# A three-layer CIN on one core: the matmuls of zeros at the start are removed

## The chip, the cores and the metric

The kernel runs on one core of one Trainium2 chip. The metric is device time in microseconds (us) of one execution; lower is better. The kernel before takes 562.39 us, the median of three runs that lie between 562.30 and 562.44 us.

## The reference

A compressed interaction network (CIN) over 512 examples, 39 fields and embeddings of 16. Each layer multiplies the original fields with the current maps, pair by pair, and contracts all pairs with a weight tensor:

```python
for idx, (W, b) in enumerate(params):                      # three layers, 128 outputs each
    z = jnp.einsum('bhd,bkd,hks->bsd', x0, xk, W) + b[None, :, None]
    z = jax.nn.relu(z)
    if idx != n_layers - 1:
        half = z.shape[1] // 2
        xk = z[:, :half, :]                                # 64 maps go on
        direct.append(z[:, half:, :])                      # 64 go to the output
    else:
        direct.append(z)
logit = jnp.sum(jnp.concatenate(direct, axis=1), axis=-1)  # sum over the 16
```

All data is float32. The einsum has 39 x 39 pairs in layer 0 (780 distinct ones) and 39 x 64 in layers 1 and 2.

## The kernel before, in words

**Tiling.** The 512 x 16 columns are cut into 16 chunks of 512 columns. For one chunk and one layer, VectorE (DVE) forms products of a field with a map, 128 pairs on the partitions by 512 columns, and TensorE (PE) contracts these 128 rows with 128 x 128 weights into the PSUM tile z. Two such tiles form a "couple". Layer 0 has seven tiles, so four couples, the last with a single tile; layers 1 and 2 have 20 tiles, ten couples each.

**Kinds of couples.** A couple is of kind E (exact), S or D (split). For E, DVE writes float32 products to the ring `exact` of four places, and PE multiplies them in float32; the profile shows each such 512-column matmul of a tile as two weight loads and two matmul records, so a couple is four records. For S and D the products are split into a high and a low part by ScalarE (ACT) and by GpSimd (POOL) or DVE, and PE runs three faster matmuls for a tile. Chunk 0 is nearly all E, and so are the first two couples of layer 0 of chunk 1 (`EARLY = 2`).

**Order of work.** Each engine has its own list of instructions, and semaphores between them. PE contracts, in order: layer 0 of chunk 0 (four couples), the two early couples of layer 0 of chunk 1, then for each chunk c layer 1 of c, the last couples of layer 2 of chunk c-1, layer 0 of chunk c+1, and layer 2 of c. Once layer 0 of a chunk is contracted, ACT applies bias and ReLU (lines 675 and 679) and writes the maps twice; only then can DVE form the products of layer 1.

**The start.** SP issues the loads of the fields (line 337) and of the weights of layer 0 (line 358), and ACT issues one part of these weights (line 699). DVE sums the two halves of the weights of layer 0 as they land (line 476), and forms the products of couple 0 and couple 1 between those sums (line 426). PE waits for each couple's products with `exact_ready`, and for `w0_summed`.

**What the change touches.** `WARM = 3` (line 72), the semaphore `warm_ready` (line 255), a memset of the tile `final` by DVE (line 479), and in PE's list ahead of the first contraction a wait and three float32 matmuls of that tile with itself, all zeros, into `z[2]` (lines 618 to 620). Their result is used by nobody: the first real matmul into `z[2]` starts a new accumulation. `final` is next written by ACT at line 696, late in chunk 1.

Of the kernel before, what the change touches and what calls it, by code (L numbers as in the profile page):

```python
# [7 lines left out]
OUT = 128  # L8
# [60 lines left out]

WEIGHT_CUTS = (0, 4, 8, 12, 16, TILES)  # L70
WEIGHTS_AHEAD = 1
WARM = 3

SUM_LAST_AT = 6
SUM_DIRECT_AT = 6
# [134 lines left out]
def cin_kernel(nc, x_fields, x_spread, w0, w1, w2, b, out):  # L210
# [7 lines left out]
    with ctx:  # L218
        def sb(name, shape, dt=fp32):
            return ctx.enter_context(nc.sbuf_tensor(name, shape, dt))  # L220

        def pb(name, shape):
            return ctx.enter_context(nc.psum_tensor(name, shape, fp32))

        def sem(name):
            return ctx.enter_context(nc.semaphore(name))
# [15 lines left out]
        final = sb("final", [128, COLS])  # L242
# [5 lines left out]
        z = [pb(f"z{n}", [128, COLS]) for n in range(3)]  # L248
# [3 lines left out]
        d_raw = pb("d_raw", [128, 2, COLS])  # L252

        w0_loaded = [sem(f"w0_loaded{p}") for p in range(W0_PARTS)]
        warm_ready = sem("warm_ready")
        w0_summed = sem("w0_summed")
        w_loaded = [None] + [[sem(f"w{n}_loaded{p}") for p in range(len(WEIGHT_CUTS) - 1)] for n in (1, 2)]
        weights_hi = [sem(f"weights{n}_hi") for n in range(3)]
# [27 lines left out]
        def wait_contracted(engine, layer, c):  # L286

            what, _, _, k = LAST_STEP[layer, c]
            if what == "exact":
                engine.wait_ge(exact_used, PLACE[E][layer, c, k] + 1)  # L290
            else:
                engine.wait_ge(lo_used, USED[layer, c, k] + 1)
# [99 lines left out]
        def _(dve):  # L392
# [83 lines left out]
                nc.vector.tensor_tensor(w_exact[0][:, a:e, :], w0_staged[:, a:e, 0, :], w0_staged[:, a:e, 1, :],  # L476
                                        ALU.add).then_inc(w0_summed, 1)

            nc.vector.memset(final[:, :], 0.0).then_inc(warm_ready, 1)
            for p in range(W0_PARTS):  # L480
                sum_weights0(p)
                multiply(0, 0, range(p, p + 1))
# [26 lines left out]
        def _(pool):  # L509
# [13 lines left out]
            def weights_split_lo(n, tiles):  # L523

                while split[n] < len(RUNS[n]) and RUNS[n][split[n]][1] < tiles:
                    _, a, e = RUNS[n][split[n]]
                    split[n] += 1
                    m = SPLIT_TILES[n].index(a)
                    e = min(e, TILES - 1)
                    pool.wait_ge(weights_hi[n], split[n])  # L530
                    nc.gpsimd.tensor_tensor(w_lo[n][:, m:m + e - a, :], w_exact[n][:, a:e, :],  # L531
                                            w_hi[n][:, m:m + e - a, :].bitcast(fp32),
                                            ALU.subtract).then_inc(weights_lo[n], 1)
# [24 lines left out]
        def _(pe):  # L558
            def contract(layer, c, couples):
                for step in SCHEDULES[SEGMENTS.index((layer, c, couples))]:  # L560
# [21 lines left out]
                    if layer and c <= 1:  # L582
                        if what == "exact":
                            pe.wait_ge(w_loaded[layer][k // 2], 16)
                        elif what == "hi":
                            pe.wait_ge(weights_lo[layer], 1 + [a <= 2 * k < e for _, a, e in RUNS[layer]].index(True))
                            if k == COUPLES[layer] - 1:
                                pe.wait_ge(weights_last_lo[layer], 1)
# [25 lines left out]
                    if what != "hi":  # L614
                        mm.then_inc(exact_used if what == "exact" else lo_used, 1)


            pe.wait_ge(warm_ready, 1)
            for _ in range(WARM):
                nc.tensor.matmul(z[2][:, :], final[:, 0:OUT], final[:, :], start=True, stop=True)  # L620
            contract(0, 0, range(COUPLES[0]))
            contract(0, 1, range(EARLY))
            for c in range(CHUNKS):
# [152 lines left out]
```

## Time and profile before

| | |
|---|---|
| median of the runs (562.30 to 562.44) | 562.39 us |
| the profiled execution's own time | 562.33 us |
| its span, first to last instruction | 560.5 us |
| TensorE busy | 551.9 us, 98% |
| VectorE busy | 535.9 us, 96% |
| GpSimd busy | 499.5 us, 89% |
| ScalarE busy | 379.4 us, 68% |
| share of TensorE in the chain that ended last | 82% |

The profile shows one execution. PE stands for matmuls, PEld for weight loads, which run beside them; SPq and ACTq are DMA issues. A "record" is one line of PE or PEld; the start of a matmul is measured, its end is modelled and includes the time in which the array drains, so two neighbours overlap a little. The pace of a stretch is therefore read from the distance between starts. Idle time that stands in brackets behind an instruction is what its engine was idle just before it, and the arrow names what ended the wait.

### The profile page before, as it was taken

The numbers are of one execution on the slowest core, as the hardware profiler recorded it, in microseconds if no ns is written. First come the engines' busy times: TensorE is split into PE (matmuls) and PEld (weight loads), VectorE is DVE, ScalarE is ACT, GpSimd is POOL, SyncE is SP. The second block draws the span as 40 slices with busy tenths as digits, with TensorE's granted clock in tenths as the row PEclk, the third lists the DMA queues.
The fourth block names the chain that finished last, engine by engine and source line by source line (L and its number), as shares of the span: only waits on it lengthen the run. The fifth ranks groups of instructions, "written<-read, shape, count | busy, mean of one in ns | idle before, by whom it ended". The sixth has DMA issues, their size and how long they took to land.

```text
span 560.5 us, 6190 instructions
## 1 busy us (share of the span) xinstructions
PE 551.9 (98%) x2008; PEld 374.9 (67%) x2008; DVE 535.9 (96%) x496; ACT 379.4 (68%) x427; POOL 499.5 (89%) x228
## 2 busy tenths in 40 slices
PE   7999999999999999999999999999999999999997
PEld 2435667667677677777767677677777767677665
DVE  4679999999999999999999999999999999999985
ACT  0436577776858767676776858777676876858662
POOL 0438899899999989999899999989999899999986
PEclk9999999999999999999999999999999999999999
DMA  8997391844828266391845828276391845826200
GB/s 326 418 408 317 132 370 34 325 191 181 344 87 331 108 254 271 146 361 30 331 183 183 342 95 333 98 262 263 150 363 29 333 177 192 333 99 215 81 1 20
DMA packets 21056, 122.17 MB, mean 218 GB/s; under 512 B 2720, under 2 KB 2976, under 8 KB 10784
## 3 DMA queue, kind: packets, MB, share of 16 engines
q1 hardware_dynamic: 20736, 121.51, 56.0%
q8 instruction: 16, 0.26, 0.2%
q10 hardware_dynamic: 288, 0.26, 0.2%
q14 instruction: 16, 0.13, 0.1%
HBM read 121.24 MB, written 0.52 MB: 217 GB/s over the span
## 4 chain that ended last, share of the span: by engine, by line
PE 82%; DVE 10%; issue 3%; ACT 2%; DMA 1%; POOL 1%; SPq 0%; DVEq 0%; POOLq 0%; ACTq 0%
PE z L611 82%; DVE raw L426 4%; DVE exact L426 3%; DVE d_raw L426 2%; DMA fields<-x_fields 1%; DVE lo L440 1%; POOL lo L515 1%; ACT hi L656 1%; ACT maps L675 0%; ACT final L696 0%; ACT L675 0%; DVE sums L453 0%; DVE sums L447 0%; SPq L358 0%; SPq L337 0%
## 5 line engine op out<-in xcount | busy, mean ns | idle before, releaser
L515 POOL TENSOR_TENSOR lo<-raw,hi 128x1024 fp32r<-128x1024 f32 x198 | 469.1, 2410 | 12.1 <-ACT hi L656 11.6
L656 ACT ACTIVATE hi<-raw 128x1024 fp32r<-128x1024 f32 (+1 forms) x213 | 219.1, 1029 | 125.1 <-DVE raw L426 112.0
L611 PE MATMUL z<-hi,w_hi 128*128 128x512 f32 (+1 forms) x559 | 220.8, 399 | 0.9 <-ACT hi L656 0.4
L426 DVE TENSOR_TENSOR raw<-spread,maps 128x1024 f32<-128x1024 f32 x184 | 219.0, 1210 | 2.1 <-ACT maps L675 2.1
L611 PE MATMUL z<-hi,w_lo 128*128 128x512 f32 x513 | 202.5, 395 | 0.0
L611 PE MATMUL z<-lo,w_hi 128*128 128x512 f32 x544 | 196.7, 451 | 0.2 <-POOL lo L515 0.2
L611 PE MATMUL z<-exact,w_exact 128*128 128x512 f32 (+1 forms) x386 | 180.4, 594 | 2.8 <-DVE exact L426 2.0
L611 PEld LDWEIGHTS z<-lo,w_hi 128*128 128x128 f32 x544 | 101.2, 188 | 56.2 <-issue 31.5
L611 PEld LDWEIGHTS z<-hi,w_hi 128*128 128x128 f32 (+1 forms) x559 | 104.8, 188 | 31.4 <-ACT final L696 3.7
L611 PEld LDWEIGHTS z<-exact,w_exact 128*128 128x128 f32 (+1 forms) x386 | 72.1, 189 | 68.0 <-issue 53.7
L611 PEld LDWEIGHTS z<-hi,w_lo 128*128 128x128 f32 x513 | 96.2, 188 | 22.9 <-issue 0.5
L426 DVE TENSOR_TENSOR exact<-spread,maps 128x1024 f32<-128x1024 f32 x76 | 91.4, 1212 | 8.2 <-ACT maps L675 5.7
L656 ACT ACTIVATE hi<-d_raw 128x1024 fp32r<-128x1024 f32 x74 | 75.8, 1025 | 21.5 <-DVE d_raw L426 18.7
L440 DVE TENSOR_TENSOR lo<-d_raw,hi 128x1024 fp32r<-128x1024 f32 x74 | 89.9, 1215 | 0.0
L426 DVE TENSOR_TENSOR d_raw<-spread,maps 128x1024 f32<-128x1024 f32 x60 | 73.3, 1221 | 0.5
L675 ACT ACTIVATE maps<-z,bias 64x512 f32<-64x512 f32 x64 | 41.5, 648 | 3.4 <-PE z L611 2.2
L515 POOL TENSOR_TENSOR hi<-raw,hi 12x512 fp32r<-12x512 f32 x15 | 19.2, 1279 | 18.5 <-ACT hi L656 18.4
L531 POOL TENSOR_TENSOR w_lo<-w_exact,w_hi 128x512 fp32r<-128x512 f32 (+3 forms) x10 | 9.9, 1001 | 22.7 <-ACT w_hi L665 22.7
L426 DVE TENSOR_TENSOR raw<-fields,copies 76x512 f32<-76x512 f32 (+1 forms) x29 | 27.1, 934 | 0.0
L679 ACT ACTIVATE direct<-z,bias 64x512 f32<-64x512 f32 x32 | 21.9, 685 | 0.8
L426 DVE TENSOR_TENSOR exact<-fields,copies 128x1024 f32<-128x1024 f32 x15 | 18.2, 1212 | 0.0
L426 DVE TENSOR_TENSOR d_raw<-fields,copies 128x1024 f32<-128x1024 f32 x14 | 17.1, 1222 | 0.0
(21 smaller groups left out, 69.6 us busy)
## 6 DMA issues: line engine op xcount, KB each, us to landing
spread<-x_spread SPq DMA_DIRECT2D x80, 1024.0 KB, 8.1
fields<-x_fields SPq DMA_DIRECT2D x31, 768.0 KB, 6.8
fields<-x_fields SPq DMA_DIRECT2D x15, 512.0 KB, 5.6
w_exact<-w SPq DMA_DIRECT2D x10, 256.0 KB, 14.7
spread<-x_fields SPq DMA_DIRECT2D x1, 768.0 KB, 10.1
raw<-w SPq DMA_DIRECT2D x1, 640.0 KB, 6.7
spread<-x_fields SPq DMA_DIRECT2D x1, 512.0 KB, 10.7
out<-sums SPq DMA_DIRECT2D x2, 240.0 KB, 4.2
```

The costliest lines, as they stand in the source:

```text
L426: nc.vector.tensor_tensor(products, by_field, by[0:rows, :].unsqueeze(1).to_broadcast([rows, tiles, COLS]), ALU.mult).then_inc(ready, 1)
L440: nc.vector.tensor_tensor(low_part(layer, c, k), d_raw[low_rows(layer, k), 0:tiles_in(layer, k), :], hi[low_rows(layer, k), place % HI_RIN ...
L515: nc.gpsimd.tensor_tensor(low_part(layer, c, k), raw[low_rows(layer, k), PLACE[S][layer, c, k] % RAW_RING, 0:tiles_in(layer, k), :], hi[lo ...
L531: nc.gpsimd.tensor_tensor(w_lo[n][:, m:m + e - a, :], w_exact[n][:, a:e, :], w_hi[n][:, m:m + e - a, :].bitcast(fp32), ALU.subtract).then_ ...
L611: mm = nc.tensor.matmul(z_of(layer, c)[:, :], w[0:rows, :], part[0:rows, :], start=(step == FIRST_STEP[layer, c] and p == 0), stop=(step = ...
L656: nc.scalar.activation(hi[0:rows, count % HI_RING, 0:tiles, :], products, ACT.Copy).then_inc(hi_ready, 1)
L675: nc.scalar.activation(maps[half * HALF:(half + 1) * HALF, :], z_of(n, c)[0:HALF, :], ACT.Relu, bias=bias[0:HALF, n:n + 1]).then_inc(evacu ...
L679: nc.scalar.activation(direct[n * HALF:(n + 1) * HALF, c % 2, :], z_of(n, c)[HALF:OUT, :], ACT.Relu, bias=bias[HALF:OUT, n:n + 1]).then_in ...
```

## The change

The three matmuls of zeros go, with the wait ahead of them, the memset that fills the tile, its semaphore, and the constant. Nothing else is changed, and nothing is put in their place: PE's first instructions are now the waits and weight loads of couple 0 of layer 0.

```diff
@@ -69,7 +69,6 @@
 WEIGHT_CUTS = (0, 4, 8, 12, 16, TILES)
 WEIGHTS_AHEAD = 1
-WARM = 3
@@ -252,7 +251,6 @@
         w0_loaded = [sem(f"w0_loaded{p}") for p in range(W0_PARTS)]
-        warm_ready = sem("warm_ready")
         w0_summed = sem("w0_summed")
@@ -476,7 +474,6 @@
-            nc.vector.memset(final[:, :], 0.0).then_inc(warm_ready, 1)
             for p in range(W0_PARTS):
                 sum_weights0(p)
                 multiply(0, 0, range(p, p + 1))
@@ -614,10 +611,6 @@
-
-            pe.wait_ge(warm_ready, 1)
-            for _ in range(WARM):
-                nc.tensor.matmul(z[2][:, :], final[:, 0:OUT], final[:, :], start=True, stop=True)
             contract(0, 0, range(COUPLES[0]))
             contract(0, 1, range(EARLY))
```

## Rows read from the trace of the kernel before

**Rows 1.** The page: busy time, share of the span, instructions of each engine.

```profile
PE 551.9 (98%) x2008; PEld 374.9 (67%) x2008; DVE 535.9 (96%) x496; ACT 379.4 (68%) x427; POOL 499.5 (89%) x228
```

**Rows 2.** The page: chain of work that ended last, its share by engine.

```profile
PE 82%; DVE 10%; issue 3%; ACT 2%; DMA 1%; POOL 1%; SPq 0%; DVEq 0%; POOLq 0%; ACTq 0%
```

**Rows 3.** All waits of TensorE's matmuls: us in total, times, longest.

```profile
PE z L611 <- DVE exact L426: 2.0, 3, 1.1
PE z L620 <- DVE final L479: 1.5, 1, 1.5
PE z L611 <- issue: 0.8, 1, 0.8
PE z L611 <- ACT hi L656: 0.4, 2, 0.2
PE z L611 <- ACT final L696: 0.4, 1, 0.4
PE z L611 <- POOL lo L515: 0.2, 1, 0.2
```

**Rows 4.** Line 620, the zeros: ns min/median/max of a record, first and last start.

```profile
L620 PE MATMUL z<-final x6: 1004/1061/1222, 1.5 to 5.9; 128*128 128x512 f32 x6
```

**Rows 5.** Timeline (start, us, instruction, idle before): weight loads of zeros, first and last.

```profile
1.45 0.50 PEld L620 LDWEIGHTS z<-final 128*128 128x128 f32 x2 [1.45 <-DVE final L479]
...
4.17 0.34 PEld L620 LDWEIGHTS z<-final 128*128 128x128 f32 x1 [0.52 <-issue]
...
5.03 0.34 PEld L620 LDWEIGHTS z<-final 128*128 128x128 f32 x1 [0.52 <-issue]
```

**Rows 6.** Timeline, 6 to 16 us: DVE's products and PE's weight loads.

```profile
6.73 1.22 DVE L426 TENSOR_TENSOR exact<-fields 128x1024 f32<-128x1024 f32 x1
...
8.00 0.30 PEld L611 LDWEIGHTS z<-exact,w_exact 128*128 128x128 f32 x2 [2.63 <-DVE exact L426]
...
8.54 0.19 PEld L611 LDWEIGHTS z<-exact,w_exact 128*128 128x128 f32 x1 [0.24 <-issue]
8.96 0.19 PEld L611 LDWEIGHTS z<-exact,w_exact 128*128 128x128 f32 x1 [0.24 <-issue]
...
10.44 0.30 PEld L611 LDWEIGHTS z<-exact,w_exact 128*128 128x128 f32 x2 [1.28 <-DVE exact L426]
...
12.30 0.30 PEld L611 LDWEIGHTS z<-exact,w_exact 128*128 128x128 f32 x2 [0.71 <-DVE exact L426]
...
12.91 2.53 DVE L426 TENSOR_TENSOR exact<-spread 128x1024 f32<-128x1024 f32 x2
...
14.22 0.29 PEld L611 LDWEIGHTS z<-exact,w_exact 12*128 12x128 f32 x2 [0.76 <-DVE exact L426]
15.27 0.30 PEld L611 LDWEIGHTS z<-exact,w_exact 128*128 128x128 f32 x2 [0.76 <-issue]
```

**Rows 7.** Chain of work in order of time: start, us, what; 15 to 41 us.

```profile
15.43 1.28 ACT L675
...
21.57 15.61 PE z L611 x38
...
38.57 2.35 DVE exact L426 x2
```

**Rows 8.** Waits of DVE in the first 60 us: total, times, longest.

```profile
DVE exact L426 <- DMA spread<-x_spread: 2.4, 3, 0.8
```

**Rows 9.** Windows: busy (x) of PE, PEld, DVE, ACT, POOL, then clock, DMA, GB/s.

```profile
1.45:2.00 0.55, 0.55 (x1) 0.50 (x2) 0.00 (x0) 0.00 (x0) 0.00 (x0) 1.00 0.84 134
...
4.00:4.50 0.50, 0.50 (x2) 0.33 (x1) 0.00 (x0) 0.00 (x0) 0.00 (x0) 1.00 1.01 397
...
5.50:6.00 0.50, 0.50 (x2) 0.00 (x0) 0.00 (x0) 0.00 (x0) 0.00 (x0) 1.00 0.96 349
...
9.00:10.00 1.00, 0.98 (x3) 0.15 (x1) 0.84 (x1) 0.00 (x0) 0.00 (x0) 1.00 1.04 436
```

## Prediction

> **What bounds the kernel now.** I read the page's busy times first: TensorE is busy for 98% of the span and VectorE for 96% [rows 1]. Two engines so near to full leave it open which of them sets the end, so the chain of waits comes next: 82% of it is TensorE, 10% VectorE, 1% DMA [rows 2]. Then I asked for everything that TensorE's matmuls waited for over the whole span. It is little: the six rows sum to 5.3 us, of which 1.5 us lie ahead of the zeros themselves [rows 3]. The reader is to see two things there. First, from the first real matmul on, TensorE has 3.8 us of idle time in 550, so what is lost on it early has almost nowhere to be made up. Second, 2.0 us of the 3.8 are three waits for VectorE's exact products, and two of them stand ahead of couples 0 and 1 (at 8.00 and 10.44 us [rows 6]), just where the change acts. So the question is how much of a loss at the start these gaps take up.
>
> Last I read the start in order of time. The zeros begin at 1.45 us and their last record begins at 5.9 us [rows 4]. The first real weight load is at 8.00 us; it waits for the product that VectorE started at 6.73 us and needed 1.22 us for, and that came as late as it did because of the first loads [rows 6]. The zeros do not delay it: TensorE has streamed the last of them more than a microsecond earlier (at 6.75 us, worked out below).
>
> **What the zeros are for, by the rows.** Their weight loads stand 0.86 us apart (4.17 and 5.03) [rows 5], those of the first real couple 0.42 to 0.43 us apart (8.54 and 8.96) [rows 6]. It is the same instruction with the same shape, 128 x 512 in float32. A factor of two is the distance of TensorE's two clock levels, 1.2 and 2.4 GHz. So the zeros ran at the low level throughout, and everything from 8.00 us on at the high one. The column of the granted clock shows 1.00 in this stretch as well [rows 9]; it contradicts the pace of the records, and I go by the pace. Between 1.45 and the rise TensorE did nothing but the zeros; without them it will have done nothing at all when couple 0 comes, and the forecast is that the low level is then met by real work.
>
> **The change part by part.**
>
> *The memset* (VectorE, line 479) goes. It runs while VectorE waits for the first weights, and is not missed: zero on both sides, as the next VectorE instruction is ended by a DMA.
>
> *The three matmuls and their wait.* They run beside the first loads, and their going frees nothing that anybody waits for: zero by themselves. What they cost when gone is the clock.
>
> *How long the low level will last.* Call it C, counted from the first matmul. From the trace: with the zeros it lasted at least until the last record had streamed, 5.9 + 0.85 = 6.75 us, so C is at least 6.75 - 1.45 = 5.3 us; and it was over at 8.00, so C is at most 6.55 us. In these 5.3 us the engine worked without a gap. The real couples will do the same at the low level, as one couple then takes 4 x 0.85 = 3.4 us and VectorE delivers a couple in 1.2 us. That makes 5.3 a fair value, and I take it, the end where the trace last saw the low level.
>
> *What a microsecond at the low level costs.* A record takes 0.85 us in place of 0.43: half of C is lost. With 5.3 us that is 2.65 us of TensorE.
>
> *What the gaps take up.* If TensorE ran at the high level without a gap from 8.00 us on, couple 0 would take 0.11 + 4 x 0.43 = 1.82 us (the 0.11 is the first load, 8.54 - 8.00 - 0.43), couple 1 1.71, couple 2 1.81 (now 14.22 - 12.30 = 1.92, less the 0.11 of a load that would be prefetched) and couple 3, of one tile, 15.27 - 14.22 = 1.05 [rows 6]. That is 6.39 us, so the next couple would start at 14.39 and not at 15.27. The difference, 0.88 us, is the slack: TensorE now waits for couple 1 until 10.44 and for couple 2 until 12.30, and with a slower TensorE both are ready before they are wanted. So the end of layer 0 of chunk 0 moves by
>
> C / 2 - 0.88 = 2.65 - 0.88 = 1.77 us (2.40 us with C = 6.55).
>
> Step by step for C = 5.3: couple 0 at the low level until 11.5 us, couple 1 starts there and is caught by the rise at 13.3, ends near 14.1, couple 2 near 15.9, couple 3 near 17.0; 17.04 - 15.27 is again 1.77.
>
> *Who waits for that.* At 15.43 us ACT begins with the load of its table and the maps, then VectorE forms the first products of layer 1, and at 21.57 us TensorE starts a stretch that has no gap until 37.2 us [rows 7]. All of this hangs on the end of layer 0 and moves with it. The two early couples stand behind couple 3 on TensorE; they fill the time until the maps come, and move too.
>
> *What could take some of it back.* VectorE waits for loads of `x_spread` three times in the first 60 us, 2.4 us in all [rows 8]. These waits shrink if VectorE comes later. But TensorE has no gap in that stretch, so a shrunken wait there gives nothing back: zero, and at most 0.4 us if the small wait ahead of 21.57 and its neighbours partly go. The loads themselves could slip: the second early product needs a place of `exact` that couple 1 frees. VectorE starts it now at about 14.2 us (12.91 and half of 2.53) [rows 6], and couple 1 would be done at 14.1 plus the draining; SP's next loads of `x_spread` stand behind that product and slip by 0.1 to 0.4 us while their users slip by 1.8. No cost. Of the other waits of TensorE, 1.8 us in all, the longest is 0.8 us [rows 3]; each is tied to its own results by way of ACT, VectorE or GpSimd; a shift leaves them as they are, and passes through.
>
> *The sum.* The profiled execution took 562.33 us, of which 560.5 are the span and 1.8 lie around it; these don't change. 562.33 + 1.77 = 564.10. The median shown is 0.06 above that execution, so 564.16, which I round to 564.2 us, 0.3% above the median of before.
>
> The Trainium skill, on the page "TensorE: Matmul & The Clock Gate", in Part 1 on the clock gate, says that the number of matmuls that run at the low level differs from run to run of one kernel, and warns against fitting a particular count. One trace can neither confirm nor deny it here. By it, 5.3 us is one draw and not a constant; where another draw would leave the sum is the first rival.
>
> **The rivals.**
>
> *The rise comes earlier than the zeros showed.* The zeros may have started at an unlucky moment. The price is the same formula. It falls to 1.1 us, the edge of what can be told from no change, at C = 4.0 us, and with C = 2.5 it is 0.4 us, 562.8 us. For it: nothing in the trace says that the low level lasts equally long whenever the work starts. Against it: the four executions of before lie within 0.14 us of each other, so whatever varies had no effect there; but the slack of 0.88 us would have hidden up to 1.8 us of low clock after 8.00 us from them.
>
> *The rise is not tied to the zeros at all.* The clock could rise some 6 us after launch, whatever TensorE does. Then the first couple at 8.00 finds the high level, and the time stays at 562.4. The rows can't exclude it, since they show only one rise and it follows on both. The same page of the Trainium skill ties the level to how busy the array has been, and speaks against this.
>
> *Faster, by better loads.* The zeros read SBUF while the first loads are written. The core's DMA moved 349 GB/s from 5.5 to 6 us and 436 GB/s from 9 to 10 us [rows 9]. If the zeros' reads were the cause, the first stretch could run up to a quarter faster, and couple 0, which waits for these loads, could start up to 1.3 us earlier, at 6.7 us: some 561.1 us if the clock rose on its own, and still 562.9 if it did not. It takes both mechanisms together for a faster kernel, and couple 0 must come at least 1.1 us earlier to be seen. Against it: from 4 to 4.5 us, with the zeros running, the rate is 397 GB/s [rows 9], already near the later one.
>
> *Worse than the formula.* The low level lasts longer since the real work has small stalls between couples, or chunk 1 falls into another rhythm; 565.2 us with 3 us lost.
>
> **How the numbers follow.** No change is what lies within 0.2%, 1.1 us, of 562.4. The forecast (C from 4.0 to 6.6 us, 563.5 to 564.8) gets 0.63; the early rise 0.24; a clock that rises by itself 0.06; faster by loads and clock 0.03; worse 0.04. So slower 0.67, same 0.29 (the early rise nearly whole, the own rise, a bit of the faster case), faster 0.04. The range leaves out little at either end: 562.5 is where the early rise costs next to nothing, 565.0 is the upper bound of C with half of the worse case.
>
> **What would show it.** In the changed kernel's timeline the weight loads after 8.00 us stand 0.85 us apart and fall to 0.43 us somewhere between 12 and 14.6 us; the waits of TensorE for couples 1 and 2 (at 10.44 and 12.30) are gone; ACT's table load begins at about 17.2 in place of 15.43, and the long stretch of 21.57 at about 23.3; from there to the end every row is later by the same 1.8 us. The forecast is wrong if the loads after 8.00 are 0.43 us apart from the first, if the rise comes within 4 us, or if the shift at 21.57 isn't found again at the end.

## The result, and the profile after

Without the zeros the kernel takes 563.84 us, the median of 13 runs, against 562.43 us for the kernel before over as many runs. The difference of the medians is 1.41 us (0.25%); the ratio of the times is 1.0021, with a 95% interval from 1.0012 to 1.0030. So it is slower: a small change, and clear of the noise, as the interval leaves out 1. Disturbed runs, one of 3171.4 us here and one of 604.66 us of the kernel before in a later round, are left out of every ratio and range in this document. Two things stand behind the medians. Without the zeros the runs lie between 562.83 and 564.57 us, a spread of 1.74 us. Of the 13 runs of before, nine lie between 562.28 and 562.44 us and four between 563.00 and 563.19.

The profiled execution took 563.48 us, 1.15 us more than the one of before. First the weight loads of its first couples (start, us, instruction, idle before and what ended it), which answer to [rows 5, 6]:

```profile
7.99 0.50 PEld L608 LDWEIGHTS z<-exact,w_exact 128*128 128x128 f32 x2 [7.99 <-DVE exact L424]
9.00 0.34 PEld L608 LDWEIGHTS z<-exact,w_exact 128*128 128x128 f32 x1 [0.52 <-issue]
9.85 0.34 PEld L608 LDWEIGHTS z<-exact,w_exact 128*128 128x128 f32 x1 [0.52 <-issue]
10.71 0.34 PEld L608 LDWEIGHTS z<-exact,w_exact 128*128 128x128 f32 x1 [0.52 <-DVE exact L424]
11.56 0.34 PEld L608 LDWEIGHTS z<-exact,w_exact 128*128 128x128 f32 x1 [0.52 <-issue]
12.29 0.19 PEld L608 LDWEIGHTS z<-exact,w_exact 128*128 128x128 f32 x1 [0.39 <-issue]
12.72 0.19 PEld L608 LDWEIGHTS z<-exact,w_exact 128*128 128x128 f32 x1 [0.24 <-issue]
...
16.43 0.30 PEld L608 LDWEIGHTS z<-exact,w_exact 128*128 128x128 f32 x2 [0.76 <-DVE exact L424]
```

The loads start 0.85 us apart and change to 0.43 between 11.56 and 12.29. That one step of 0.73 us holds both paces, and dates the change: a time y at the low level costs y/2 extra, so y = 2 x (0.73 - 0.43) = 0.6, and the change falls at 12.16 us. The low level lasted C = 12.16 - 7.99 = 4.2 us of real work. (C is the word of the prediction: how long the low level lasts, counted from the first matmul.) The waits ahead of couple 1 and couple 2 are gone, and the load of the first early couple stands at 16.43, 1.16 us after its place before (15.27 [rows 6]).

Next TensorE's waits over the whole span, to be set beside [rows 3], and the chain of waits in order of time (start, us, what), beside [rows 7]:

```profile
PE z L608 <- DVE exact L424: 8.4, 2, 8.0
PE z L608 <- issue: 0.8, 1, 0.8
PE z L608 <- ACT hi L649: 0.4, 2, 0.2
PE z L608 <- ACT final L689: 0.4, 1, 0.4
PE z L608 <- POOL lo L512: 0.2, 1, 0.2
```

```profile
7.99 8.53 PE z L608 x14
...
16.59 1.28 ACT L668
...
22.74 15.61 PE z L608 x38
...
39.73 2.35 DVE exact L424 x2
```

Of the 2.0 us that TensorE waited for VectorE's exact products from 8.00 us on, 0.4 are left (8.4 less the 8.0 ahead of the first matmul); every other wait from there on is the same to the tenth. And every piece of the chain is late by the same amount: ACT's table by 1.16, the long stretch by 1.17 (its length is 15.61 as before), VectorE by 1.16. The last long stretch of TensorE in the chain tells that next to nothing was given back in 500 us. Here are both kernels, the one before first; its stretch began at 545.87, the one of after at 547.01, 1.14 later:

```profile
545.87 11.40 PE z L611 x41
```

```profile
547.01 11.40 PE z L608 x41
```

### The profile page after: what moved, and what is told of

Its sections match the earlier page's. It is cut to its first block, busy times and chain, and to the rows that moved or that the text cites. A ratio compares the mean times of both kernels' runs of the same rounds, so it can differ in the third digit from the quotient of the medians.

```text
span 561.7 us, 6177 instructions
## 1 busy us (share of the span) xinstructions
PE 548.1 (98%) x2002; PEld 374.2 (67%) x2002; DVE 535.4 (95%) x495; ACT 379.5 (68%) x427; POOL 499.5 (89%) x228
## 4 chain that ended last, share of the span: by engine, by line
PE 83%; DVE 10%; issue 3%; ACT 2%; DMA 1%; POOL 1%; DVEq 0%; POOLq 0%; ACTq 0%
PE z L608 83%; DVE raw L424 4%; DVE exact L424 3%; DVE d_raw L424 2%; DVE lo L438 1%; DMA raw<-w 1%; POOL lo L512 1%; ACT hi L649 1%; ACT maps L668 0%; ACT final L689 0%; ACT L668 0%; DVE sums L451 0%; DVE sums L445 0%; DVE w_exact L474 0%; ACT w_hi L658 0%
```

## The experiments

**A fourth matmul of zeros.**

```diff
-WARM = 3
+WARM = 4
```

> The kernel before with four matmuls of zeros in place of three, so that TensorE works without a gap from 1.45 us into couple 0. Theory (the rise of the clock follows on matmul work, and where in that work it comes differs from execution to execution): of 13 executions of the kernel before four took 563.0 to 563.2 us, 0.7 us more than the others; these are the ones in which three zeros ended before the rise, and a fourth closes the gap: all executions near 562.4, none above 562.8. In executions with a late rise the fourth zero ends near 8.3 us and delays couple 0 by 0.3 us, which the wait for couple 1 takes up. Rival (the 0.7 us have nothing to do with the clock, they are some other mode of the kernel): about a third of the executions stay near 563.1. Rival (every delay of couple 0 is paid): all executions 0.2 to 0.3 us above 562.4.

Measured: 562.49 us at the median, 11 runs from 562.22 to 562.58, against 562.42 for the kernel before; ratio 0.9997 (0.9988 to 1.0006), so no change at the median. But none of the 11 lies above 562.6, while 8 of the 31 runs of the kernel before beside them lie between 563.04 and 563.31. The profile shows the rise between the loads at 4.18 and 4.79 us here, 2 us before that of [rows 5]:

```profile
3.32 0.34 PEld L620 LDWEIGHTS z<-final 128*128 128x128 f32 x1 [0.52 <-issue]
4.18 0.34 PEld L620 LDWEIGHTS z<-final 128*128 128x128 f32 x1 [0.52 <-issue]
4.79 0.19 PEld L620 LDWEIGHTS z<-final 128*128 128x128 f32 x1 [0.28 <-issue]
...
7.91 0.30 PEld L611 LDWEIGHTS z<-exact,w_exact 128*128 128x128 f32 x2 [2.07 <-DVE exact L426]
8.44 0.19 PEld L611 LDWEIGHTS z<-exact,w_exact 128*128 128x128 f32 x1 [0.24 <-issue]
```

The rise is at 4.18 + 2 x (0.61 - 0.43) = 4.54 us, so C is 3.1 us. The same work from the same 1.45 us met the rise at quite different points: the place of the rise varies from execution to execution. A delay of couple 0 could not be seen in this one, since its zeros were done early. The expectation took the runs above 563 for a late rise; what they are is told below, and it is something else.

**Two matmuls of zeros.**

```diff
-WARM = 3
+WARM = 2
```

> The kernel before with two matmuls of zeros in place of three: TensorE works from 1.45 to 4.9 us and is then idle for 3.1 us until couple 0 comes. Theory (the rise needs work without a long gap ahead of it, and an idle stretch puts the clock back): near the kernel without zeros, 563.4 to 563.9 us at the median, with weight loads of couple 0 standing 0.85 us apart. Rival (the work ahead of the gap counts in full): 562.4 to 562.8, with loads of couple 0 already 0.43 us apart or the rise within its first two records.

Measured: 563.15 us at the median, eight of the 11 runs between 562.96 and 563.20, the others 563.21, 563.88 and 564.42; ratio 1.0014 (1.0005 to 1.0023). That is below the range that the theory named (563.4 to 563.9) and above that of the rival. The reason stands in the windows of the profile, which took 563.05 us (last three columns: granted clock, share of the DMA engines, GB/s):

```profile
4.00:8.00 4.00, 0.91 (x2) 0.00 (x0) 1.59 (x3) 0.00 (x0) 0.00 (x0) 0.98 1.00 380
8.00:8.50 0.50, 0.48 (x1) 0.49 (x2) 0.50 (x1) 0.00 (x0) 0.00 (x0) 0.50 1.05 430
...
10.00:11.00 1.00, 1.00 (x3) 0.48 (x2) 0.46 (x1) 0.00 (x0) 0.00 (x0) 0.50 1.05 436
11.00:11.50 0.50, 0.50 (x2) 0.13 (x2) 0.39 (x1) 0.00 (x0) 0.00 (x0) 0.72 0.99 418
11.50:12.00 0.50, 0.50 (x3) 0.26 (x2) 0.50 (x1) 0.00 (x0) 0.00 (x0) 1.00 0.99 414
```

The clock fell to 0.50, the 1.2 GHz level, just ahead of couple 0 (the mean of 0.98 up to 8.00 has the fall in it), after TensorE had done nothing since 4.9 us, and stayed there until past 11 us. By the loads:

```profile
8.01 0.50 PEld L611 LDWEIGHTS z<-exact,w_exact 128*128 128x128 f32 x2 [4.36 <-DVE exact L426]
...
10.74 0.34 PEld L611 LDWEIGHTS z<-exact,w_exact 128*128 128x128 f32 x1 [0.52 <-DVE exact L426]
11.44 0.19 PEld L611 LDWEIGHTS z<-exact,w_exact 128*128 128x128 f32 x1 [0.37 <-issue]
...
16.02 0.30 PEld L611 LDWEIGHTS z<-exact,w_exact 128*128 128x128 f32 x2 [0.76 <-DVE exact L426]
```

The change falls at 10.74 + 2 x (0.70 - 0.43) = 11.28, C is 3.3 us, and 16.02 is 0.75 us late. So in this execution two zeros brought the rise, and the idle stretch behind them lost it again. Eight of the 11 runs, those from 563.05 to 563.21, have the same mean granted clock on record, 0.997; the other three (562.96, 563.88, 564.42) have 1.0. What is left of the zeros' use is that the low level on the real work was shorter here, 3.3 us against the 4.6 us that the median without zeros stands for; at the medians they save 0.69 of the 1.41 us.

**The memset and the wait without the matmuls.**

```diff
             pe.wait_ge(warm_ready, 1)
-            for _ in range(WARM):
-                nc.tensor.matmul(z[2][:, :], final[:, 0:OUT], final[:, :], start=True, stop=True)
```

> The memset, its semaphore and TensorE's wait for it are kept, and only the three matmuls of zeros are gone. Theory (all of the loss is the clock at couple 0): the same as the changed kernel, 563.4 to 564.2 us at the median, a spread of 1.5 us or more between executions, loads of couple 0 at 0.85 us. Rival (the memset or TensorE's early wake-up plays a part): within 0.2 us of 562.4, or at least 0.5 us off the changed kernel.

Measured: 563.96 us, 10 runs from 562.98 to 564.40; ratio 1.0023 (1.0014 to 1.0033), within 0.12 us of the changed kernel's median, and with a spread of 1.42 us (a little under the 1.5 expected). No part of the memset can be seen. The profiled execution, of 564.11 us, had a longer low level:

```profile
7.95 0.50 PEld L611 LDWEIGHTS z<-exact,w_exact 128*128 128x128 f32 x2 [7.95 <-issue]
...
13.23 0.27 PEld L611 LDWEIGHTS z<-exact,w_exact 128*128 128x128 f32 x1 [0.52 <-issue]
13.74 0.19 PEld L611 LDWEIGHTS z<-exact,w_exact 128*128 128x128 f32 x1 [0.24 <-issue]
...
17.03 0.30 PEld L611 LDWEIGHTS z<-exact,w_exact 128*128 128x128 f32 x2 [0.76 <-issue]
```

The change falls at 13.23 + 2 x (0.51 - 0.43) = 13.39, so C is 5.4 us, and the shift is 17.03 - 15.27 = 1.76.

**One zero, straight ahead of couple 0.**

```diff
-WARM = 3
+WARM = 1
             pe.wait_ge(warm_ready, 1)
+            pe.wait_ge(w0_loaded[0], 16)
```

> One matmul of zeros in place of three, and TensorE waits for the first part of the weights of layer 0 (landed at 6.36 us) before it, so that it runs from 6.4 to about 8.1 us, straight ahead of couple 0. Theory (the time at the low level counts from the first matmul, and half of what falls on real couples is lost): 1.7 us of the low level fall on the zero and 0.15 us go as couple 0 starts later; with the 4.6 us that the median of the changed kernel (1.4 us lost, slack 0.88) stands for, the loss is (4.6 - 1.75) / 2 - 0.88 + 0.15 = 0.7 us, 563.1 us at the median, between 562.4 and 563.8. Rival (only an early start helps, or the clock rises some time after launch whatever is done): 563.8 like the changed kernel, or 562.4 like the kernel before.

Measured: 562.79 us, 11 runs from 562.25 to 563.60; ratio 1.0005 (0.9996 to 1.0013). The median is 0.3 us under the expected 563.1 and the spread is the expected one (562.4 to 563.8). By the medians a single zero at the right place takes back 1.05 of the 1.41 us, and two early ones 0.69; the intervals of the two ratios overlap, so which is better is not certain. The profile (562.73 us), the zero first:

```profile
6.43 0.50 PEld L621 LDWEIGHTS z<-final 128*128 128x128 f32 x2 [6.43 <-issue]
...
8.30 11.07 PE L611 MATMUL z<-exact,w_exact 128*128 128x512 f32 x22
...
10.01 0.34 PEld L611 LDWEIGHTS z<-exact,w_exact 128*128 128x128 f32 x1 [0.52 <-issue]
10.66 0.19 PEld L611 LDWEIGHTS z<-exact,w_exact 128*128 128x128 f32 x1 [0.32 <-DVE exact L426]
...
15.67 0.30 PEld L611 LDWEIGHTS z<-exact,w_exact 128*128 128x128 f32 x2 [0.76 <-DVE exact L426]
```

The change falls at 10.01 + 2 x (0.65 - 0.43) = 10.45, so C is 4.0 us. Couple 0 starts at 8.30, 0.19 late against 8.11 (the 8.00 of before and the 0.11 of its first load), and 2.15 us of it are at the low level: 1.08 + 0.19 - 0.88 = 0.39, and the early couple is 0.40 us late.

**Eight matmuls of zeros.**

```diff
-WARM = 3
+WARM = 8
```

> The kernel before with eight matmuls of zeros, so that the whole low level falls on zeros and couple 0 is only late. Theory (the start has a slack of 0.88 us, all beyond it is paid in full, and the clock has no other price): with a low level of 4.2 us counted from 1.45 the 16 records end at 1.45 + 0.11 + 16 x 0.43 + 2.1 = 10.5 us; TensorE is 2.5 us late for couple 0, and the end moves by 2.5 - 0.88 = 1.6 us, 564.0 us, with 563.5 to 564.8 as the low level is shorter or longer. In the profile the shift of the load at 15.27 and that of the end agree within 0.1 us. Rival (there is no such slack): 564.9. Rival (later stages take a late start up, and only the clock hurts): 562.4.

Measured: 563.46 us, nine runs from 563.20 to 564.60; ratio 1.0023 (1.0013 to 1.0032). That is 0.5 us under the 564.0 expected and just outside its range; by the same formula the median stands for a low level of 3.3 us, where the expectation took 4.2. In the profile (563.96 us) all real work runs at the high level and only comes late:

```profile
5.88 0.23 PEld L620 LDWEIGHTS z<-final 128*128 128x128 f32 x1 [0.52 <-issue]
6.35 0.19 PEld L620 LDWEIGHTS z<-final 128*128 128x128 f32 x1 [0.24 <-issue]
...
10.64 9.99 PE L611 MATMUL z<-exact,w_exact 128*128 128x512 f32 x22
...
16.93 0.30 PEld L611 LDWEIGHTS z<-exact,w_exact 128*128 128x128 f32 x2 [0.76 <-issue]
```

The rise is at 5.88 + 2 x (0.47 - 0.43) = 5.96, and the zeros had the low level for 4.5 us. The first real matmul starts at 10.64, 2.53 us late against 8.11, and the early couple 16.93 - 15.27 = 1.66; the difference, 0.87, is the slack by itself, without the clock. It was worked out as 0.88. The end moved by 1.63 (563.96 - 562.33). Both rivals, no slack and everything taken up, fall.

**ACT's table loaded early, with four zeros and with none.** The chain spends 1.28 us on the load of ACT's table between layer 0 and the maps [rows 7]. Apart from what it may bring, it moves the start in the other direction.

```diff
+        scrap = sb("scrap", [128, 1])
...
             act.wait_ge(bias_loaded, 16)
+            nc.scalar.activation(scrap[:, :], bias[:, 0:1], ACT.Relu, bias=bias[:, 0:1])
             spread_maps1(0)
```

> Four matmuls of zeros, and one ReLU of the bias, a single column, into a tile of its own at the start of ACT's work, so that ACT's table is loaded while it waits for layer 0, and not between layer 0 and the maps (1.28 us on the chain of the kernel before). Theory (a shift of the start passes through to the end in either direction): the maps come 1.28 us earlier; TensorE has to finish the two early couples first (their end at about 18.9 us becomes the bound, a gain of 0.4 us at the load of 19.35) and then runs on without the waits of 0.4 and 0.2 us ahead of 21.57, so that this stretch starts about 0.8 us earlier: 561.6 us. Rival (the table is not what ACT waits for, or it is loaded again): 562.4. Rival (a gain at the start is lost to the loads, which are due soon after): 562.1 to 562.4, with TensorE waiting for VectorE's products between 23 and 31 us.

> The changed kernel, without zeros, with the same early ReLU for ACT's table. Theory (the clock's loss and the table are two terms that add up): 0.8 us below the changed kernel's 563.8, so 563.0 us, and 1.4 us above the kernel with four zeros and the early table. Rival (the early table leaves room for the late TensorE, and takes the loss up): 562.4 or below.

Measured: 561.68 us with four zeros (11 runs, 561.49 to 561.75; ratio 0.9985, 0.9977 to 0.9994; before 562.34), and 562.81 us with none (11 runs, 561.61 to 563.28; ratio 1.0004, 0.9995 to 1.0013). The first is the best version that was run: under the kernel before by 0.66 us, an interval clear of 1, and free of its runs above 563. The chain of its profile shows a stretch of TensorE that starts at 20.94 in place of 21.57, 0.63 earlier:

```profile
20.94 15.60 PE z L612 x38
```

Half of the 1.28 us was lost at the first product of layer 1:

```profile
15.38 1.32 ACT L676 ACTIVATE maps<-z,bias 64x512 f32<-64x512 f32 x2 [7.05 <-PE z L612]
17.44 1.22 DVE L427 TENSOR_TENSOR exact<-spread,maps 128x1024 f32<-128x1024 f32 x1 [2.00 <-ACT direct L680]
```

The maps are written by 16.70, but VectorE starts at 17.44. The profile puts that wait down to ACT's line 680, which wrote another tile, `direct`; in the kernel before the same product starts at 18.08, when that instruction has only begun. This product also needs the first load of `x_spread`, and by the landings in the trace that load was complete at 17.36, which fits. VectorE's waits of the first 60 us, to be set beside [rows 8], show the next of these loads too:

```profile
DVE exact L427 <- DMA spread<-x_spread: 3.2, 4, 0.8
```

There are now four waits for `x_spread` and 3.2 us of them, where three took 2.4. In the kernel before the first of these loads is complete at 17.35, so it is some 0.7 us ahead of its use, and a start that comes earlier by more than that meets it.

The version without zeros is 1.03 us under the changed kernel and 1.13 above its partner, where 0.8 and 1.4 were expected. Its profile (563.08 us) shows that the two terms do not simply add:

```profile
7.90 30.11 PE z L609 x64
...
546.72 11.30 PE z L609 x41
```

```profile
13.19 0.33 PEld L609 LDWEIGHTS z<-exact,w_exact 128*128 128x128 f32 x1 [0.52 <-issue]
13.96 0.19 PEld L609 LDWEIGHTS z<-exact,w_exact 128*128 128x128 f32 x1 [0.44 <-issue]
...
17.25 0.30 PEld L609 LDWEIGHTS z<-exact,w_exact 128*128 128x128 f32 x2 [0.76 <-issue]
```

The change falls at 13.87, so C is 6.0 us, and the early couple is 1.98 us late, as C / 2 - 0.88 has it (2.1). But TensorE then works from 7.90 to 38.0 us without a gap, and its last long stretch starts 1.45 us behind the one with four zeros (545.27). So half a microsecond of the 1.98 was taken up: TensorE's waits between the early couples and the long stretch, 0.4 and 0.2 us in the kernel before, are gone. So the rival (the early table leaves room for a late TensorE) holds in part, and the table is worth more where TensorE is late.

**The kernel before, looked at again.** Four more profiled executions of it, unchanged.

> The kernel before once more, for a second look at its start; a quarter of its executions take 563.0 to 563.3 us, and the question is what stands in those. If this one takes 562.4: weight loads of couple 0 at 0.43 us. If it takes 563.1: theory (the clock is low on real work in these too): some loads after 8.00 us stand 0.85 us apart, over some 3.2 us, as (563.1 - 562.4 + 0.88) x 2 = 3.2; rival: loads at 0.43 us throughout and the 0.7 us lost elsewhere.

> The kernel before, once more with a profile. About a fifth of its executions take 563.0 to 563.3 us in place of 562.4, and the question is what stands in one of those. With two zeros the clock rose early, fell again at the first real couple, and the execution took 563.05. Theory (the same happens here): when the rise comes early, the zeros end sooner, the idle stretch before 8.00 us grows from 1.2 to over 2 us, the clock falls soon after 8.00 and the real weight loads stand 0.85 us apart for some 3.3 us. Rival (the rise came late): the zeros run at the low level to their end, and so do the first real records. If the execution takes 562.4 it tells nothing on this.

> As the look before it: the same kernel, and the same two theories for an execution of about 563.1 us.

> As the two looks before it: the same kernel, and the same two theories for an execution of about 563.1 us.

Measured: 562.30, 562.34, 562.40 and 562.38 us. All four show real loads at 0.43 us from the first on, and none is of the slower kind (15 of 70 runs of this kernel are: 4 of 13, 8 of 31 and 3 of 26). They do show once more that the rise moves. The six records of line 620 (ns min/median/max), third look first, then the fourth:

```profile
L620 PE MATMUL z<-final x6: 1061/1061/1222, 1.5 to 5.9; 128*128 128x512 f32 x6
```

```profile
L620 PE MATMUL z<-final x6: 593/1061/1219, 1.5 to 5.9; 128*128 128x512 f32 x6
```

In the third look all six are long, so the low level lasted to the end of the zeros; in the fourth the last one is short (593 ns, as a real record at the high level), so the clock had risen by 5.9 us and C was at most 4.4 us.

What stands in the executions of 563.1 us was not seen in a profile, but the mean granted clock of every execution beside the experiments is on record, and it settles the kind. That mean leaves out the low level ahead of the first rise: it is 1.0 for the changed kernel's profiled execution with its 4.2 us, and 0.997 for the one with two zeros, in which the clock fell after a rise. Of the 57 runs of the kernel before that stood beside the experiments and were not disturbed, the 11 between 562.95 and 563.31 all show 0.997, and the 46 others (562.20 to 562.54) 0.999 or 1.0. So the slower kind is an execution in which the clock rose and fell again, and not one in which it rose late. The lost 0.003 of some 561 us stands for about 3.4 us at half the clock; C / 2 - 0.88 makes 0.8 us of that, and these runs are 0.6 to 0.9 us longer than the rest. With a fourth zero, which shortens the idle stretch, none of 22 runs has it (11 of the kernel with four zeros, 11 with the table besides). That the fall stands at couple 0, as with two zeros, is argued from this cost and not shown.

## Why the prediction was right, point by point

- **The mechanism** (the low level met by real work, half of it lost, less the slack) holds in every profiled execution whose real work met the low level. With C read from the loads, C / 2 - 0.88 gives 1.20, 0.75 and 1.84 us for the changed kernel, two zeros and the memset alone; the early couple was late by 1.16, 0.75 and 1.76, and the execution was longer than the one of before by 1.15, 0.72 and 1.78.
- **The slack of 0.88** was measured by itself with eight zeros: 0.87.
- **The shift passes through.** 1.16 us at the load of 16.43, 1.14 at the last stretch. VectorE's waits for `x_spread` shrank from 2.4 to 1.6 us in the first 60 us, as expected, and gave nothing back.
- **The size.** 564.2 was forecast and 563.84 measured, a loss of 1.8 against 1.41 us. The term that was too large is C: 5.3 us, taken from the one execution with zeros, where the low level in fact ended within the last record (1004 ns against 1061 of those before it [rows 4]). By the same formula the runs stand for 4.6 us at the median (2 x (1.41 + 0.88)) and for 2.6 to 6.0 at the ends (562.83 and 564.57); in the profiled execution it was 4.2. What was called a bound there was a bound for that one execution; other profiled executions with zeros from the same 1.45 us had C of 3.1 and 4.5 us. The slower runs are the forecast and the faster ones its first rival, the early rise: one kernel, a mixture of both. That the forecast came within 0.4 us is partly luck: one draw from a range of 2.6 to 6.0 us did not fall at an end of it. By its own signs it was close, too. The rise was to come between 12 and 14.6 us, and not within 4 us of the first matmul; in the profiled execution it came at 12.16, after 4.2 us. Why one execution gets 3 us and another 6 stays open.
- **One thing was not thought of:** that a rise can be lost again before the real work. It does not touch the changed kernel, but it makes about a fifth of the runs of the kernel before 0.7 us longer. The prediction's argument that before's runs agree within 0.14 us rested on four runs.
- **The chances** hold a slip: "faster" got 0.04, but the one rival that makes it faster has 0.03. Nothing hangs on it.
- **The rise by itself** is refuted: the rise lay before 8.00 us with zeros and at 12.16, 13.39 and 10.45 us where the first matmul came at 7.99, 7.95 and 6.43.
- **Faster by better loads** is refuted. Without zeros VectorE's first sum starts at 6.37 us and the first real load at 7.99, where it was 6.38 and 8.00.

The Trainium skill, on the page "TensorE: Matmul & The Clock Gate", in Part 1, says that the count of matmuls at the low level is different from run to run. The spread of 1.74 us without zeros, against 0.16 us of the common runs with three, agrees, as does the fourth zero's rise 2 us earlier.

## What to carry to other kernels

Matmuls of zeros that fill the time of the first loads are worth half of the low-clock time they take off the real work, less the gaps in which that work waits anyway; here 1.4 us of 562 at the median, and a spread of 0.9 us where it is 1.7 without them. They have to reach up to the first real matmul: two early ones followed by 3 us of idleness kept half of the gain, one right ahead of the work three quarters of it by the medians, and with eight the work came late and the gain was gone. A fall of the clock in executions that were never profiled can be found in the mean granted clock of each run. Before taking such a term from one trace, ask whether what ends it (here the rise of the clock) is at the same place in the next execution.

## What the runs showed of the hardware that was not expected

- The granted clock fell back to 0.50 after 3 us without matmuls (from 4.9 to just ahead of 8.0 us) and stayed there until past 11 us, with two zeros. In the profiled executions with three and four zeros TensorE was idle for 1.1 to 1.5 us ahead of couple 0, and its loads stood 0.43 us apart from the first on. The 11 runs of before with a mean clock of 0.997 say that the fall comes with three zeros as well. How long TensorE was idle in those is not known; if the rise came at 4.5 us, as in the profile with four zeros, its six records would have ended at about 5.8, which leaves 2.2 us (an estimate from that profile's rows).
- The column of the granted clock shows 1.00 ahead of the first rise, where the loads of the zeros stand 0.85 us apart; after the first rise it agreed with the loads in the profile with two zeros. The distance of the weight loads tells the level throughout.
- ACT's table load of 1.28 us came onto the chain because it ran only when TensorE's layer 0 was done (15.43 [rows 7]). With one ReLU of a single column placed earlier in ACT's work it ran at 1.66 us, although that ReLU itself waited for the bias until 8.04:

```profile
1.66 1.28 ACT L703 ACT_TABLE_LOAD   x1 [1.66 <-PEq L769]
8.04 0.29 ACT L703 ACTIVATE scrap<-bias 128x1 f32<-128x1 f32 x1 [5.10 <-DMA bias<-b]
```
